# Four groups of batch rows in each turn of the loop, in place of two

## The reference, cut to what matters

```python
x = x + mixer(_layernorm(x))                  # state-space mixer: in_proj, causal conv of 4 taps, silu,
                                              # softplus step size, scan over the 128 tokens for 1024 channels
                                              # times 16 states, gate, out_proj
x = x + attention(_layernorm(x), ctx_2048)    # 8 heads of 16, a band of 64 tokens to either side, over the
                                              # 512 features as positions; relu, times ctx, w_ct
x = x + experts(_layernorm(x))                # 8 experts of width 16, the best 2 of them by a router
return x
```

## Time and profile before

| | |
|---|---|
| median of 3 runs | 5532.19 us (5530.11 to 5533.7) |
| profiled execution, its own time | 5533.42 us |
| span of the profile | 5531.6 us |
| granted TensorE clock, mean | 0.964 |
| TensorE busy | 4796.2 us (87%) |
| VectorE busy | 4955.4 us (90%) |
| ScalarE busy | 4058.8 us (73%) |
| GpSimd busy | 4541.5 us (82%) |
| fetches of instructions | 416 on DMA queue 8 (6.82 MB), 229 on queue 14 (1.87 MB) |

### The profile page before, as it was taken

The page is one execution under the profiler, slowest core; times in us unless marked ns, Lnnn a source line. Parts: engine busy times, 40 slices in busy tenths (PEclk is TensorE's granted clock), DMA queues, the critical chain, the costliest instruction groups (busy, mean ns, idle before and its releaser), DMA issues.

```text
span 5531.6 us, 139169 instructions
## 1 busy us (share of the span) xinstructions
PE 4796.2 (87%) x51012; PEld 3435.7 (62%) x51012; DVE 4955.4 (90%) x7075; ACT 4058.8 (73%) x7812; POOL 4541.5 (82%) x3464
## 2 busy tenths in 40 slices
PE   5788888988888988888989888989888988898876
PEld 3566666666666666666666666666666666666653
DVE  3999999999999999999999999999999999999972
ACT  3677777877777777777877777777777777777752
POOL 2988888888888888888888888888888888888870
PEclk8899999999999999999999999999999999999986
DMA  3211222221212221212221222221212221221100
GB/s 112 71 63 42 70 68 74 70 66 42 74 64 74 70 67 41 74 64 74 71 67 40 74 64 74 74 70 34 77 64 70 74 74 38 70 69 66 62 9 11
DMA packets 114693, 350.19 MB, mean 63 GB/s; under 512 B 13057, under 2 KB 14849, under 8 KB 113921
## 3 DMA queue, kind: packets, MB, share of 16 engines
q1 hardware_dynamic: 114048, 341.51, 19.0%
HBM read 323.64 MB, written 17.83 MB: 62 GB/s over the span
## 4 chain that ended last, share of the span: by engine, by line
PE 46%; DVE 18%; issue 15%; POOL 11%; ACT 7%; DVEq 1%; POOLq 0%; ACTq 0%
POOL ring L300 7%; PE ps L1066 7%; PE ps L1114 6%; DVE ring L1454 5%; PE ps L1096 5%; PE ps L982 4%; PE ps L957 4%; POOL ring L309 4%; PE ps L1134 3%; PE ps L1010 3%; DVE nmax L1489 3%; ACT ps L462 3%; DVE ring L1439 2%; DVE tmp L1423 2%; PE ps L1021 1%
## 5 line engine op out<-in xcount | busy, mean ns | idle before, releaser
L300 POOL TENSOR_TENSOR ring<-du,bc 128x512 f32<-128x512 f32 x2048 | 2741.9, 1356 | 577.7 <-PE ps L1066 352.3
L1454 DVE TENSOR_TENSOR_SCAN ring<-ps,ring 128x512 f32<-128x512 f32 x2048 | 2456.7, 1211 | 201.2 <-POOL ring L300 103.1
L462 ACT ACTIVATE ps<-delta,a_neg 128x254 f32<-128x254 f32 x4096 | 1761.5, 468 | 326.9 <-DVE ring L1454 320.9
L309 POOL TENSOR_TENSOR ring<-ring,bc 128x512 f32<-128x512 f32 x1280 | 1776.5, 1394 | 232.5 <-DVE ring L1454 230.6
L1066 PE MATMUL ps<-ident,ring 128*128 128x128 f32 x8192 | 1103.7, 282 | 73.7 <-DVE ring L1439 43.1
L1066 PEld LDWEIGHTS ps<-ident,ring 128*128 128x128 f32 x8192 | 962.9, 145 | 193.5 <-issue 119.1
L1439 DVE TENSOR_TENSOR ring<-ring,bc 128x512 f32<-128x512 f32 x768 | 755.4, 987 | 3.4
L592 ACT ACTIVATE probs_mem<-ps 128x768 f32<-128x768 f32 (+1 forms) x512 | 455.9, 911 | 176.0 <-PE ps L1010 174.4
L1134 PE MATMUL ps<-w_in,xt_a 128*128 128x256 f32 x2048 | 488.8, 394 | 12.8 <-DVE hc L1582 8.1
L1114 PE MATMUL ps<-xt_a,w_in 128*128 128x256 f32 x2048 | 476.6, 386 | 7.1 <-DVE hc L1582 4.1
L1096 PE MATMUL ps<-w_outp,yz 128*128 128x512 f32 x1024 | 462.5, 599 | 18.7 <-ACT yz L526 18.7
(11 more groups left out here) (136 smaller groups left out, 6362.2 us busy)
## 6 DMA issues: line engine op xcount, KB each, us to landing
w_in<-in_w_in SPq DMA_DIRECT2D x256, 512.0 KB, 3.7
bc<-bc_rows SPq DMA_DIRECT2D x256, 512.0 KB, 4.1
x_new<-in_x SPq DMA_DIRECT2D x32, 512.0 KB, 6.2
x_res<-in_x SPq DMA_DIRECT2D x32, 512.0 KB, 5.5
enc<-in_ctx SPq DMA_DIRECT2D x64, 256.0 KB, 5.3
out<-x_att SPq DMA_DIRECT2D x32, 512.0 KB, 2.8
w_outp<-in_w_outp SPq DMA_DIRECT2D x1, 2048.0 KB, 8.0
bc_rows<-bc_sb SPq DMA_DIRECT2D x32, 32.0 KB, 1.5
```

The lines of the kernel that those rows point to most:

```text
L300: nc.gpsimd.tensor_tensor(ring[:, s % RING, :].rearrange("p (n t) -> p n t", n=2), du[:, q % 2, (ic % 2) * NT:(ic % 2 + 1) * NT].rearrange ...
L309: nc.gpsimd.tensor_tensor(ring[:, s % RING, :], ring[:, s % RING, :], bc[:, s % RS, 2:4, :].rearrange("p a t -> p (a t)"), ALU.mult).then_ ...
L462: nc.scalar.activation(ps[:, s % DAR, (n % 2) * NT:(n % 2 + 1) * NT].rearrange("p (b t) -> p b t", b=GB)[:, :, 1:T], delta[:, ic, :].rearr ...
L1454: nc.vector.tensor_tensor_scan(ring[:, s % RING, :], ps[:, s % DAR, :], ring[:, s % RING, :], 0.0, ALU.mult, ALU.add).then_inc(h_done, 1)
```

## The change

In the loop of each of the five engines the bounds and the body change. The step is 4, the upper bound NG - 4 = 28, and the body is four passes. g takes the values 2, 6, ..., 26, so there are 7 turns and they cover groups 2 to 29. The passes behind the loop are the same as before. The hint and the head's place are kept as they were, and SP still has neither.

```diff
-            with nc.Fori(2, NG - 2, 2, engines=bass.OrderedEngineSet([sp.engine])) as g:
+            with nc.Fori(2, NG - 4, 4, engines=bass.OrderedEngineSet([sp.engine])) as g:
                 iteration(g, True, True, True, True)
                 iteration(g + 1, True, True, True, True)
+                iteration(g + 2, True, True, True, True)
+                iteration(g + 3, True, True, True, True)
             iteration(NG - 2, True, True, True, True)
...
-            with nc.Fori(2, NG - 2, 2, engines=bass.OrderedEngineSet([pool.engine]), hint_back_edge=True,
+            with nc.Fori(2, NG - 4, 4, engines=bass.OrderedEngineSet([pool.engine]), hint_back_edge=True,
                          head_slot={pool.engine: 0}) as g:
                 iteration(g, True, True, True, True)
                 iteration(g + 1, True, True, True, True)
+                iteration(g + 2, True, True, True, True)
+                iteration(g + 3, True, True, True, True)
             iteration(NG - 2, True, True, True, True)
```

More of the change, by code:

```diff
@@ L872, in _ @@
             iteration(1, True, True, True, False)
-            with nc.Fori(2, NG - 2, 2, engines=bass.OrderedEngineSet([act.engine]), hint_back_edge=True,
+            with nc.Fori(2, NG - 4, 4, engines=bass.OrderedEngineSet([act.engine]), hint_back_edge=True,
                          head_slot={act.engine: 0}) as g:
@@ L1374, in _ @@
             iteration(1, True, True, True, False)
-            with nc.Fori(2, NG - 2, 2, engines=bass.OrderedEngineSet([pe.engine]), hint_back_edge=True,
+            with nc.Fori(2, NG - 4, 4, engines=bass.OrderedEngineSet([pe.engine]), hint_back_edge=True,
                          head_slot={pe.engine: 0}) as g:
@@ L1834, in _ @@
             iteration(1, True, True, True, False)
-            with nc.Fori(2, NG - 2, 2, engines=bass.OrderedEngineSet([dve.engine]), hint_back_edge=True,
+            with nc.Fori(2, NG - 4, 4, engines=bass.OrderedEngineSet([dve.engine]), hint_back_edge=True,
                          head_slot={dve.engine: 0}) as g:
```

## The result

The changed kernel takes 5544.1 us (median of 18 runs, 5538.5 to 5551.7), the one before 5532.9 (18 runs beside them): a ratio of 1.002 with an interval of 1.0013 to 1.0028, so about 11 us slower, and clear of noise (I had taken 11 us for the least that can be told). I had forecast 5531.6 and no measurable change. The time lies inside the range that I gave, 5522 to 5545, but at its upper end and by luck: what moved it there is not what I had widened the range for.

The account below looks back on a forecast made before the run. It took the common pace of VectorE, GpSimd and TensorE, handing groups round, as the bound. Jumps -0.6, entry and exit 0, code streams 0, work 0 took the median 5532.2 to 5531.6 us, range 5522 to 5545.

Parts of the forecast that it names:

- what I had widened the range for: Range 5522 to 5545: widened by 4 us either side for the loop's exit, and above by a half-covered jump miss.
- The jumps cost nothing: Loop end, each engine: queued work covers a taken jump, 0.00 us on VectorE, 0.08 on TensorE, at most 0.19.
- My 0.6 us: Loop end: seven jumps fewer at TensorE's 0.08 us each save 0.6 us.
- Rival 1: Loop's jumps: hint fails over longer code, 4.0 to 4.8 us at each of 6 jumps, 5556 to 5561; chance 0.06.
- the 4.80 us: Loop's entry: VectorE's next scan starts 4.80 us late, taken as the price of code not there.
- Rival 2: GpSimd's loop: body no longer held, fetched anew each turn, slowing the ring; 5560 us named; chance 0.03.
- the bound from VectorE's and ScalarE's stream: GpSimd's loop: lower bound of nothing for new fetches, as those two engines stream straight on with groups of even length.
- code streams 0: Loop bodies: twice the code, fetched at the same rate on TensorE's queue 8, adds 0 us.
- rival 3: TensorE's clock in the loop: 12 more short groups by chance, 16 us faster, 5516; chance 0.04.
- The exit: Loop's exit: the stall stays once, its size may shift by -4 to +4 us with where the body ends; 0 taken.
- The sign of being wrong that I had named: Behind the loop: group 30 losing or gaining more than 4 us would show the forecast wrong.
- The other sign: Inside the loop: group lengths from 165.2 to 166.0 us in all four places of a turn would confirm the forecast.

Follow-up runs that it names:

- a head 17 instructions ahead of a border: Kernel before, two groups a turn, with TensorE's loop head at slot 239 of a block: 5549.2 us, ratio 1.0038.
- the best with two: Kernel before, two groups a turn, with TensorE's loop head moved to slot 128 of a block: 5522.6 us, ratio 0.9978.
- ten slots: Changed kernel with TensorE's loop head 10 instructions further into a block of code: 5531.1 us, ratio 1.0001 to the kernel before.
- slot 128: TensorE's loop head half a block further on: 5522.6 us on the kernel before, 5527.2 us on the changed kernel.

## Why the prediction was wrong

**The jumps cost nothing: right.** VectorE's step at a border with a jump is still 0.58 us (1079.28 to 1079.86 in the changed kernel). TensorE's idle there is 0.70.
```profile
1079.28 0.67 DVE L1438 TENSOR_TENSOR delta<-delta,lnv 128x512 f32<-128x512 f32 x1
1079.86 1.22 DVE L1462 TENSOR_TENSOR_SCAN ring<-ps,ring 128x512 f32<-128x512 f32 x1
```
```profile
1075.65 1.13 PE L1171 MATMUL ps<-ts,w_dt 128*128 128x256 f32 x4 [0.70 <-ACT gate_t L555]
```
With four or with seven groups a turn, no kernel beats the best with two. My 0.6 us is too small for any run here to tell.

**Rival 1, the jump misses: did not happen** in the changed kernel. Only a head 17 instructions ahead of a border made every jump costly. Of its two prices the 4.80 us was read too simply: the row puts that wait down to GpSimd's product. The changed kernel, where VectorE stands 3.81 us by issue at the same place, gives the price without that doubt.

**Rival 2, GpSimd: its mechanism came, its price did not.** I forecast some 40 fetches more on queue 14, and GpSimd's edit alone gave 39. (The changed kernel has 26 more, since VectorE's edit alone takes 14 away.) GpSimd's turn is 372 instructions before and 738 after, counted in the trace. The Trainium skill's 512 instructions held ("Runtime: NRT & Kernel Launch", section on instruction fetch mechanics) agree with that. But the bound from VectorE's and ScalarE's stream, nothing, was the right one.

**The step that failed: "TensorE ... already streams. ... The rate is the same and no row shows it to stall", with "code streams 0" in the sum.** The rate is the same; the place is not. I priced a stream by its mean, 26 fetches in 331 us, one in 13 us. But TensorE issues 128 instructions in 0.85 us where the score matmuls are, so a block of 256 would last 1.7 us there (an estimate from that run), while a fetch takes one DMA engine 0.9 us (4.6% of 16 engines over 1.2 us). There it counts how long ahead of the border the fetch ends: in the changed kernel 0.16 us lay between an idle of 0.17 us and one of 0.7. The term that I put at 0 is +10 us, by TensorE's edit alone and by what ten slots take back. I had asked that very question of the small engines ("the last block of an engine's body may be a stub") and, for TensorE, only of the exit. The Trainium skill says in the section on instruction fetch mechanics of "Runtime: NRT & Kernel Launch" that fetching is hidden because instructions are dispatched more slowly than blocks arrive; the run of 64 that breaks off for 0.71 us shows an exception.

**How the idles add up to that term is shown in part.** Seven idles of 0.7 us are 5 us, and the profile has the 26 groups from 3 to 28 longer by 4.8, but the two are not the same microseconds. The seven groups with an idle are together only 1.0 us longer than the same groups before, while groups 5, 8 and 18, with no idle over 0.2 us, are 4.8 us longer. With TensorE's edit alone, nine idles sum to 4.9 us and groups 3 to 28 are longer by 8.1. A group's length goes with where the stretches of half clock fall in it. Three patterns make up nearly all groups of the kernels without idles: one stretch of 3.4 us at some 102 us (164.0 us long), two of 3.4 at 52 and 103 (165.2), one of 6.8 at 101 (165.6 to 165.9). The groups of 166.9 to 167.4 us have one of 6.8 us at 51 to 52. Over groups 3 to 28, the four kernels with idles on the score line have 6 to 13 groups over 166 us, the ten without have 0 to 3. In group 4 of the changed kernel the stretch is at 800.3, in that of the kernel before at 847.9 (in the 3.4 us ahead of it TensorE is busy for 1.40 us and for 1.78; columns as above; clock 0.50 is 1.2 GHz, 1.00 is 2.4):
```profile
800.30:803.70 3.40, 3.40 (x32) 2.36 (x28) 3.10 (x6) 3.05 (x6) 3.26 (x4) 0.50 0.00 0
848.20:854.90 6.70, 5.14 (x32) 4.56 (x33) 6.63 (x8) 3.58 (x8) 3.65 (x4) 1.00 0.00 0
```
```profile
800.00:803.40 3.40, 2.29 (x38) 1.27 (x36) 3.17 (x6) 3.40 (x8) 3.40 (x4) 1.00 0.01 2
847.90:854.60 6.70, 6.00 (x22) 5.49 (x23) 6.67 (x9) 4.17 (x9) 3.10 (x3) 0.50 0.00 1
```
At the earlier place TensorE is busy throughout, and the group comes to 166.3 us; with the low stretch at the later one it takes 165.7. In the changed kernel's profile every group over 166 us, but the one at the exit, has a low stretch at 51 to 54 us from its start and none at some 102. I saw rival 3 as blind chance, and wrote that nothing in the change touches it. But the place of the code goes with it in both directions: long groups come with the idles, short ones with slot 128. That a stall of 0.7 us is what shifts the low stretches was not tested by itself.

**The exit: right in kind, too narrow in effect.** I took 0 between -4 and +4 for it. Groups 29 and 30 together took 334.5 us before and 336.7 after, so +2.2, and from 329.7 to 339.8 over all the kernels here. The sign of being wrong that I had named, group 30 off by more than 4 us, would not have told: it is 2.3 us shorter, and the 4.6 us are in group 29. The other sign, group lengths of 165.2 to 166.0 in all four places of a turn, did.

**Left open.** Why the fetch is made some 4 to 10 us later (at 32.4 to 33.6 us of the group, for 28.3 in first and 23.9 to 28.4 in second passes) when the border is 6 or 12 instructions later. The point from which it is asked for may have moved across a wait; no run here separates that from other reasons. Open too is why one place of the code gives the short groups in regular order, and ScalarE's possible 3 us.

## What to carry to other kernels

A change of a loop's length is a change of where all its code lies. In an engine that issues in dense runs, price the code by the densest run that a block border can fall into, not by the mean of fetches, and vary the head's slot before and after: here ten slots took back nearly all that the change had cost, and a slot alone, without the change, gave the best kernel. Testing one engine's edit at a time took four runs and found 10 of the 11 us in one of them.

## What the runs showed of the hardware that I had not expected

- A border between blocks of TensorE's code inside a run of small matmuls can stop the run for 0.4 to 0.7 us, though its 64 pairs take only 0.85 us. Whether it does hangs on when a fetch ends: in the changed kernel none at 1.06 us or more ahead of the break, all seven at 0.9 us or less.
- A head of the loop 17 instructions ahead of a block border made TensorE wait at every jump and at the exit, 23.9 us in 14 times, though the jump was hinted.
- GpSimd's 39 fetches more cost nothing that can be measured (ratio 1.0000), and VectorE's longer body nothing either (1.0004) but for the stall at the exit; for ScalarE's (1.0009, 1.0000 to 1.0018) a small loss can't be excluded.
- Two stalls of some 4 us at the loop's exit, on two engines, cost little more than one: groups 29 and 30 take 336.0 us with VectorE's stall beside TensorE's and 334.5 without.
- Groups of the same work are 164.0 to 166.9 us long in the kernel before, none of them with an idle over 0.35 us in the score runs, by where the granted clock's low stretches fall in them; and the place of the code changes how often each length comes (three groups of 164 us in 28, or nine).
